# Queries and keys projected transposed, and moved to their partitions by DMAs

## The reference

```python
# latent branch: 16 heads, 16 content + 64 rotary features each
c_q = x @ w_dq.T
q_c, q_r = c_q @ w_uq.T, c_q @ w_qr.T          # (b, 16, s, 16), (b, 16, s, 64)
c_kv = x @ w_dkv.T
k_c, v, k_r = c_kv @ w_uk.T, c_kv @ w_uv.T, x @ w_kr.T
q_r, k_r = _rope(q_r, k_r)                     # x*cos + rot(x)*sin, by token
attn = softmax(mask(concat(q_c, q_r) @ concat(k_c, k_r).T * SCALE))
s = (attn @ v) @ w_out.T
# second branch: 16 heads of 16 features, on xn = rmsnorm(x, w_ln1)
h = softmax(mask(q @ k.T / 4)) @ v
x1 = x + h @ Wo.T
ffn = x1 + moe(rmsnorm(x1, w_ln2))             # 8 experts, the top 2 of each token
out = x0 + s * silu(ffn)
```

## Time and profile before

| | |
|---|---|
| Median of 3 runs | 896.05 us (895.1 to 898.09) |
| The profiled execution | 900.06 us, its span 898.3 us |
| TensorE busy | 822.7 us, 92% of the span |
| VectorE, ScalarE, GpSimd busy | 68%, 56%, 44% |
| Mean granted clock of TensorE | 0.945 |

### The profile page before, as it was taken

One profiled execution on the slowest core, in us unless ns is written; L12 is line 12 of the kernel. 1 busy time (PEld: TensorE's weight loads), 2 busy tenths in 40 slices (PEclk: granted clock), 3 DMA queues, 4 the chain that ended last, 5 costly groups with the idle time before them and its releaser, 6 DMA issues.

```text
span 898.3 us, 18344 instructions
## 1 busy us (share of the span) xinstructions
PE 822.7 (92%) x6432; PEld 735.3 (82%) x6432; DVE 612.4 (68%) x2191; ACT 502.1 (56%) x1089; POOL 391.4 (44%) x538
## 2 busy tenths in 40 slices
PE   5889999999999999999999999988669999999980
PEld 3778988898897898888889889866459999999980
DVE  4976666767767676667776675762537878887854
ACT  2445466457347536536645744644237878787851
POOL 4632342344344344434434434414344565656640
PEclk9988999999999999999999999977769999999995
DMA  9000000000000000000000000122368999999836
GB/s 291 2 1 2 14 1 12 16 13 3 25 14 2 25 14 1 26 13 2 14 14 13 3 25 13 11 87 86 105 183 207 237 230 232 255 261 243 234 37 198
DMA packets 49871, 71.07 MB, mean 79 GB/s; under 512 B 12067, under 2 KB 36003, under 8 KB 49763
## 3 DMA queue, kind: packets, MB, share of 16 engines
q1 hardware_dynamic: 39060, 57.41, 20.8%
q0 software_dynamic: 9856, 12.13, 7.7%
q10 hardware_dynamic: 864, 0.36, 0.2%
HBM read 55.13 MB, written 14.81 MB: 78 GB/s over the span
## 4 chain that ended last, share of the span: by engine, by line
PE 76%; DVE 10%; ACT 5%; DMA 4%; issue 3%; POOL 1%; SPq 1%; POOLq 0%; ACTq 0%; DVEq 0%
PE ps L608 62%; PE ps L702 6%; PE ps L739 3%; DVE ps L1509 2%; ACT ex L1175 2%; DVE ps L1506 1%; PE ps L635 1%; DMA expert_rows<-yo,slot_of 1%; DMA ln<-in_w_ln 1%; PE ps L992 1%; PE ps L644 1%; DMA xg<-x_normalised,slot_of 1%; SPq L377 1%; DVE xr L1788 1%; DVE s_tok L1786 1%
## 5 line engine op out<-in xcount | busy, mean ns | idle before, releaser
L544 POOL TENSOR_SCALAR_AFFINE_SELECT ex<-ex 128x256 f32<-128x256 f32 x256 | 104.4, 411 | 232.1 <-ACT ex L1175 211.4
L608 PE MATMUL ps<-qt,kt 81*128 81x128 f32 (+2 forms) x768 | 166.6, 331 | 3.8 <-ACT ex L1175 2.0
L1175 ACT ACTIVATE ex<-ps 128x384 f32<-128x384 f32 x240 | 116.0, 492 | 95.0 <-PE ps L608 93.2
L522 POOL TENSOR_TENSOR ex<-ex 128x256 f32<-128x256 f32 x128 | 102.5, 801 | 110.3 <-DVE ex L1466 109.3
L1506 DVE CUSTOM_DVE_ANT_0 ps<-ps,mask 128x128 f32<-128x128 f32 x256 | 77.1, 301 | 92.2 <-PE ps L608 88.8
L608 PEld LDWEIGHTS ps<-qt,kt 81*128 81x128 f32 (+1 forms) x768 | 111.1, 197 | 15.8 <-issue 6.0
L1509 DVE CUSTOM_DVE_ANT_0 ps<-ps,mask 128x256 f32<-128x256 f32 x256 | 118.6, 463 | 0.0
L585 POOL DMA_INDIRECT expert_rows<-yo,slot_of x46 | 77.0, 1674 | 82.6 <-ACT yo L1310 55.1
L1347 DVE TENSOR_TENSOR wel<-raw,weh 128x768 fp32r<-128x768 f32 x92 | 87.7, 956 | 18.3 <-ACT weh L1045 18.3
L608 PE MATMUL ps<-wh,xth 128*128 128x320 f32 (+2 forms) x352 | 96.1, 355 | 4.4 <-DVE wl L1347 3.0
L1045 ACT ACTIVATE qt<-ps 80x512 f32<-80x512 f32 (+1 forms) x96 | 56.8, 592 | 61.5 <-PE ps L702 59.4
(11 more groups left out here) (160 smaller groups left out, 1914.3 us busy)
## 6 DMA issues: line engine op xcount, KB each, us to landing
raw<-in_w_experts SPq DMA_DIRECT2D x92, 384.0 KB, 4.5
mla_branch<-s_b SPq DMA_DIRECT2D x8, 256.0 KB, 2.1
expert_rows<-xn SPq DMA_DIRECT2D x8, 256.0 KB, 2.1
x_normalised<-otk SPq DMA_DIRECT2D x8, 256.0 KB, 2.1
xr<-in_x SPq DMA_DIRECT2D x1, 2048.0 KB, 10.4
s_tok<-mla_branch SPq DMA_DIRECT2D x4, 512.0 KB, 6.9
w_cols_raw<-in_w_cols SPq DMA_DIRECT2D x1, 1792.0 KB, 15.6
x<-expert_rows SPq DMA_DIRECT2D x3, 512.0 KB, 5.1
```

The lines of the kernel that those rows point to most:

```text
L522: nc.gpsimd.tensor_tensor(t, t, swp[:, n % 2, :, :], ALU.add).then_inc(tokd, 1)
L544: nc.gpsimd.affine_select(a, a, [[0, 2], [1, P]], ALU.is_ge, zero, 0, -1).then_inc(exm, 1)
L608: return nc.tensor.matmul(o, a, m, start=start, stop=stop, skip_group_check=True, **k)
L1175: nc.scalar.activation(ex[:, h % (2 * G), :], ps[4 + h % 2][:, P:4 * P], ACT.Exp, scale=scale).then_inc(ex_, 1)
```

## The change

Queries and keys of both branches are projected with the weights as the stationary operand, so that features lie on partitions and 256 tokens in columns; the columns of the weights are reordered on the host. A unit is now a bank of two 128-feature halves, twelve matmuls of 256 columns. There are 13 units a batch (`UNITS`): content of queries and keys (`nq`, `nk`), four rotary pairs (`q0` to `k3`, four heads each, one half of the rotary features per half bank), the multi-head ones (`mq`, `mk`), and the latent values. No transposes of queries and keys are left. Results go to five staging slots `stg`, and SP copies them from there to the partitions where `qt` and `kt` want them, a head's features on 80 partitions. The multi-head ones are scaled by the rms row, split into high and low part, stored in memory (`multi_heads`) and loaded to `qt2` and `kt2`. The first two latent maxima move into p1, and maxima in general are issued two heads ahead; the rounding for them (`qr`, `kr`, a ring of three groups) is all ScalarE's.

```diff
+UNITS = ("nq", "nk", "q0", "k0", "q1", "k1", "q2", "k2", "q3", "k3", "mq", "mk", "v")
+BANK = dict(nq=0, nk=1, q0=4, k0=5, q1=0, k1=1, q2=4, k2=5, q3=0, k3=1, mq=4, mk=5, v=0)
+STAGED = dict(nq=1, nk=1, q0=2, k0=2, q1=2, k1=2, q2=2, k2=2, q3=2, k3=2, mqh=4, mql=2, mkh=4, mkl=2)
...
+            def place_rope(b, g, a):
+                s, _, _ = place(b, "qk"[a] + str(g))
+                sp.wait_ge(tokd, 8 * b + 2 * g + a + 1)
+                for t in range(2):
+                    o = (qt, kt)[a][t * RD // 2:(t + 1) * RD // 2, G * g:G * (g + 1), :]
+                    sp.dma_start(o, stg[:, s, t, :]).then_inc(sl[s], 16)
...
+                    for k in parts:
+                        for e in range(2):
+                            sp.dma_start(mha_d[a, e, D * k:D * (k + 1), :, :].rearrange("d (j t) s -> (d j) t s", t=2),
+                                         stg[e * ST:(e + 1) * ST, s, :, :]).then_inc(sl[s], 16)
+
+            def load_mha(b, t):
+                wait(sp, st2, 16 * (b - 1) + 8 * (t + 1))
+                for name in ("mqh", "mql", "mkh", "mkl"):
+                    s, _, done = place(b, name)
+                    sp.wait_ge(sl[s], done)
+                for e in range(2):
+                    for a, o, n in ((0, qt2[:, e, :, :], ST), (1, kt2, MROW2)):
+                        sp.dma_start(o[ST * e:ST * e + n, 4 * t:4 * (t + 1), :].bitcast(F32),
+                                     mha_d[a, e, 0:n, 4 * t:4 * (t + 1), :]).then_inc(mrd[t], 16)
...
+                row2(b)
+                stage_p1(b + 1, lambda: store_s(b))
+                load_mha(b + 1, 0)
+                row1(b + 1)
+                load_mha(b + 1, 1)
...
+            def features(o, c0):
+
+                k = 0
+                for w, a in ((wh, xth), (wl, xth), (wh, xtl)):
+                    for e in range(ET):
+                        i = mm(o, w[:, e, c0:c0 + P], a[:, e, :], k == 0, k == 2 * 3 - 1)
+                        k += 1
+                return i
...
                 def head(h):
-                    if h == 0:
-                        wait(pe, t2e, 8 * b + 8)
-                        wait(pe, t2o, 4 * b + 4)
+                    if h % 8 == 0:
+                        wait(pe, mrd[h // 8], 64 * (b + 1))
...
                     scores_t(h, ps[4 + h % 2]).then_inc(st, 1)
-                    if h > 0:
-                        max_head(h - 1)
+                    if h + 2 < H:
+                        max_head(h + 2)
+                    if h == H - 1:
+                        tail()
...
+                    p1_with_m1(b + 1, {"nq": after_first, "k0": between, "k1": back, "k2": project})
+                    stage_t2(b, max1(b + 1), {5: lambda: project_v2(b + 1)})
...
+                nc.vector.tensor_tensor(stg[:, s, :, :], a, cos_t[:, :].unsqueeze(1).broadcast_to([P, 2, S]), ALU.mult)
+                nc.vector.tensor_tensor(prb[:, n % 2, :, :], a[:, ::-1, :], sin_t[:, :, :], ALU.mult).then_inc(roped, 1)
...
             def stage_p1(b, after):
+                for n in range(2 * NG):
+                    products(b, n)
                     after.get(n, lambda: None)()
+                first_m1(b)
+                mha_scale(b, 0)
+                mha_scale(b, 1)
+                mha_low(b, 0)
+                mha_low(b, 1)
```

More of the change, by code:

```diff
@@ L84, with unit, place @@
 C_OWN = C_THR
+def unit(b, name):
+    return len(UNITS) * b + UNITS.index(name) + 1
+def place(b, name):
+    n = len(STAGED) * b + list(STAGED).index(name)
+    counts = list(STAGED.values()) * (b + 1)
+    free = 16 * sum(counts[n % NS:n:NS])
+    return n % NS, free, free + 16 * counts[n]
 def wait(engine, semaphore, value):
@@ new lines, in stage_p1 @@
+            def stage_p1(b, between):
+                wait(sp, st1, 16 * b)
+                if b == 0:
+                    sp.wait_ge(wdone, N_DIRECT)
+                    sp.wait_ge(wdonep, 1)
+                    sp.wait_ge(combl, N_COMB)
+                    sp.dma_start(kt[MROW:MROW + 1, :, :], ones.rearrange("o (h t) -> o h t", h=H)).then_inc(s_one, 16)
+                place_content(b, 0)
+                place_content(b, 1)
+                for g in range(NG):
+                    place_rope(b, g, 0)
+                    place_rope(b, g, 1)
+                between()
+                for t in range(2):
+                    wait(sp, mrd[t], 64 * b)
+                store_mha(b, 0)
+                store_mha(b, 1)
@@ L593, in _ @@
                 scatter(blk)
[L595 to L600, removed]
-                if i >= 2 and (i - 2) % 9 != 8:
-                    step_tr(i - 2, 8 * ((i - 2) // 9) + (i - 2) % 9)
-                after.get(i, lambda: None)()
         @block.tensor
@@ new lines, in mha_high, with rms_rows, keep_v1 @@
+            def mha_high(b, a):
+                s, free, _ = place(b, ("mqh", "mkh")[a])
+                wait(act, sl[s], free)
+                act.wait_ge(m2p, 2 * b + a + 1)
+                copy(stg[:, s, :, :].bitcast(F32R), prb[:, a, :, :]).then_inc(hi2, 1)
+            def rms_rows(b):
+                act.wait_ge(rst, b + 1)
+                wait(act, m2p, 2 * b)
+                copy(rsb[:, :], ps[2][:, S:2 * S]).then_inc(rsd, 1)
+            def keep_v1(b):
+                act.wait_ge(p1d, unit(b, "v"))
+                wait(act, pv1, NG * b)
+                for tt in range(2):
+                    i = copy(v_heads(v1, tt)[:, :, 0:D], of_unit("v")[:, tt, :].rearrange("p (h c) -> p h c", h=H))
+                i.then_inc(v1d, 1)
```

618 lines of the change are left out of this document (296 added, 322 removed).

## The result

The changed kernel takes 861.42 us in the median of 4 runs (852.36 to 864.37). The kernel before took 897.07 beside it; the ratio is 0.958, with a 95% interval of 0.950 to 0.967. It is faster, but by less than half of what was forecast: 35.7 us of 88 in the medians. The profiled execution took 858.59 us (span 856.9) against 812.5 in the sum.

A forecast was written before the change was run, and what follows sets the result against it. TensorE bounds attention, busy 71.2 of each 72.5 us period, with t2 paced by VectorE near its end. Seven periods at -10.4 (-73), first batch -12, last -2.5: 900.06 becomes 812.5, as median 808; range 784 to 848.

The forecast's parts named there:

- p1: Stage of the projections of batch b+1, 28.40 us a period; removing its transposes was to gain 7.0 us.
- the transposes: TensorE's transposes removed by the change: 7.0 us a period in p1 and 3.5 us in p2.
- p2: Stage transposing the multi-head rows, 5.09 us a period; 3.5 us of transposes and a 0.44 us wait were to go.
- t1: Stage of latent scores of batch b with its multi-head maxima, 21.64 us a period; TensorE never waits long there.
- The DMAs of the rotary placement: Rotary placement in p1: 7.7 us against 11.7 us of other TensorE work, so hidden by 4 us.
- VectorE's and GpSimd's prices in p1: 1.2 us a unit on VectorE, 1.3 (at most 1.6) us a sum on GpSimd, both hidden behind TensorE.
- t2: Stage of multi-head scores with the next latent maxima, 17.42 us; gain 2.7 us a period, keeping 1.1 us of waits.
- two normalised tiles (1.2+0.7 us): VectorE in the first batch: 1.2 us a unit plus 0.7 for two normalised tiles; eight units end at 48.
- T0: End of the second scaling, about where t2 begins; put at 50.6 us in the first batch.
- the round trip: Multi-head data to memory and back: there at T0+13.1 to T0+15.7, costing TensorE 2.0 us of wait a period.
- Rival (a): Half-partition multi-head transfers at half rate: 864 us, 836 with partial overlap, 832 by the skill's figures; 830 to 865, chance 0.18.
- the clock ... 0.7 us each: The new 2 us wait may bring a clock fall, 1.5 us, in half of the periods: 0.7 us each.

The follow-up runs named there:

- 9: The kernel of 8 without dummy matmuls in t2 and with fewer in batch 0 (10 and 34 instead of 70 and 24): 834.76 us, ratio 0.931.
- 3: Changed kernel with ScalarE's third pair of latent casts and VectorE's low halves moved later at the start of t2: 864.01 us, ratio 0.965.
- 11: The kernel of 9 with VectorE's low halves behind the latent maxima of heads 3 and 4, nothing moved on ScalarE: 843.16 us, ratio 0.942.
- Experiment 2: Changed kernel with batch 0's normalised tiles moved from the rotary products to the first multi-head maxima: 857.18 us, ratio 0.954.
- 6: Changed kernel with dummy matmuls, changing no result, in TensorE's waits at the start of t2, batches 0 to 6: 873.08 us, ratio 0.970.
- 8: Changed kernel with normalised tiles moved, 8 stores instead of 12, query-side loads issued earlier, dummy matmuls in batch 0 and t2: 834.07 us, ratio 0.928.
- 10: The kernel of 8 with fewer dummy matmuls in batch 0 (10 and 34 instead of 70 and 24), those in t2 kept: 826.46 us, ratio 0.923.
- experiment 4: Changed kernel with each pair of multi-head stores merged into one over 128 partitions, 6 issues a batch instead of 12: 1063.0 us, ratio 1.188.

## Why the forecast was half right

**Right: the transposes and p1.** p1, p2 and t1 together fell by 8.1 us in a period without a wait. By the prediction's terms, with the second half of the multi-head projection (1.4) and two heads' maxima (0.5) moved into p1, it should be 8.5. Projections of 256 columns lie 0.118 apart. The DMAs of the rotary placement are hidden for TensorE inside p1. VectorE's and GpSimd's prices in p1 were right (1.2 and 1.3 us).

**Wrong: "t2. ... I keep 1.1 us of waits".** This is the step that failed in the periods. Its work had been counted, its first heads hadn't. The sum asked when the casts of the first group are there, not what stands behind the cast of the third on ScalarE: the split, and behind it exponentials and VectorE's low halves. The cast itself stood waiting for its placement; the prediction had asked only when that of the first group lands. These waits (1.4 us) and the clock that fell behind them made up for the work taken away. To the transposes t2 takes 15.6 us on average in the six later periods, where the prediction's terms give 11.1. In the changed kernel itself the one t2 at a clock of 1.00, that of batch 0, takes 14.1; in 9 the difference is 2 us. Orders that take single waits away (3, 11) made new ones. The shortest t2 seen in any run, 13.4 us in 9, is still 2 us over the forecast for this stretch. In it VectorE's row has hardly a gap for the first 5 us, the low halves and then six heads' maxima at 0.6 to 0.8 us each, against the 0.47 of TensorE's two pairs a head; that points to VectorE as the pace of this stretch, but no run changed that alone.

**Wrong: "two normalised tiles (1.2+0.7 us)" and T0 = 50.6.** 0.7 was the price of these tiles with GpSimd at rest. Beside its sum one of two takes 1.4 us. Experiment 2 shows it, 7.2 us. The Trainium skill ("SBUF — State Buffer", section "SBUF: two separate sides") states that GpSimd and VectorE, when VectorE runs in a two-port mode or reads two inputs from SBUF, take a shared pair of ports in turn, and that whichever starts first blocks the other for its whole instruction. The trace agrees with that, 0.41 and 1.40 us, the second tile ending just behind the sum; it doesn't show the mode.

**Mis-sized: the round trip.** With T0+17.5 it was 1.8 to 4.4 us longer than forecast at its shortest: 1.2 to the first store instead of 0.5, 9.4 from there to the first load instead of 7.5, and 6.9 from there to the last landing instead of 5.1. The issue (0.63) is inside the bounds; the value taken was too low. Rival (a) put such a delay down to the rate of half the partitions. It came nearest to the time (836 to 864) for another reason: the stores were priced at 10.4 us by it and take 7.55, and TensorE's mean wait is 1.1 us, not 9. That it has the time is luck. Whether transfers of half the partitions are slower stays open: the stores to both halves are in flight together, the loads' 6.9 us lie between the 5.1 of the forecast and the 8.2 of the rival, and no run moves the same bytes over 128 partitions on all engines. By the times that the prediction takes from the figures of the Trainium skill (8 and 4.7 us, against 5.4 of issuing and 3.0) a trip is 4.3 us longer, not 3, and the estimate 842, not 832. What the trip did is hidden in the table: t2 was just long enough to cover it, so where t2 became shorter the wait behind it grew (2, 6). A shorter t2 paid only together with a shorter trip (8, 10).

**Mis-sized: "the clock ... 0.7 us each".** A wait on `multi_heads` over 1.9 us was followed by a stage of 28.8 to 29.5 us instead of 27.95 in the changed kernel, 0.8 to 1.5, near the forecast; in 6 it was from nothing (behind 2.34 us) to 4.4. Not priced at all were the fall inside t2 and the first batch. There the change moved the idle time to just ahead of the score stage, which cost 11.3 us. Two windows of the kernel before, of which the first ends where its 32 transposes begin and the second lies in them:

```profile
66.00:72.00 6.00, 4.25 (x16) 3.00 (x15) 4.59 (x26) 1.37 (x4) 0.00 (x0) 0.50 0.00 0
76.00:78.00 2.00, 2.00 (x17) 1.76 (x16) 1.39 (x2) 1.88 (x4) 0.00 (x0) 1.00 0.00 0
```

The clock was at 0.50 there too, but it was back at 1.00 before the first scores at 77.42; now the scores themselves meet the low clock. Why it then stays low for so long isn't shown.

The Trainium skill ("TensorE: Matmul & The Clock Gate", section "HAM oscillation — how this bites in real kernels") describes waits for a DMA that make what follows start at the lower level; the trace of the first batch agrees.

Of the 46 us, then: first batch 28, of which 11 are the clock, 7 the tiles and 8 the trip and the maxima row behind it (eight loads go out before the row, which took 5.95 us to land), with some 2 unassigned; the rest t2 and the waits. The clock's and the tiles' part are shown by experiments, the division of the rest is read from one trace. The fastest version has won back 32 of the 46 (ratio 0.958 to 0.923), with loads in a new order and with dummies; the last 14 stay.

## What to carry to other kernels

When work is taken from the engine that sets the pace, ask at each stage border what its first two instructions wait for, and what stands ahead of that on the other engines; a stage shortened in its middle keeps its length through its start. Two waits can cover each other: a stage that is too long hid a transfer that was too long, and one alone could not be mended. A wait can cost more than itself, when the clock of the stage behind it falls: nothing to 4.4 us here behind waits of 1.5 to 3 us, and 11.3 us once.

## What the runs showed of the hardware

- The granted clock stood at 0.50 for 21.5 us (81.96 to 103.48) while TensorE's row shows it busy all the time. In experiment 4's first batch, behind a wait of 27 us, it was 0.50 from 106.64 to 131.50 with TensorE busy throughout; in a later batch, behind a wait of 24 us, it was back at 1.00 within 8 us (300 us on, from 291.8).
- A fall of the clock inside t2 made the same instructions take 15.4 to 16.2 us instead of 13.4 to 13.8 (experiment 9).
- An SP issue of a store from SBUF to memory took 0.42 us for 64 KB, 0.60 for 128 KB and 0.61 for 256 KB; single ones behind other stores took 1.0 to 2.1.
- An fp32 operation of VectorE on 128x256 from SBUF to SBUF took 0.41 us, and 1.38 to 1.40 where it started inside GpSimd's addition of 128x512; it ended some 0.15 us behind it.
- A transfer whose pattern begins with a dimension of 2 kept a DMA share of 0.13 and 51 GB/s; with 64 first, the same bytes ran at a share of 0.93 and 212 GB/s.
